# Causal attention in a four-block kernel: from head steps on stacked fp32r halves to query-tile steps of four heads on row groups

## What is computed

```
def _mha(x, y, wq, wk, wv, ..., causal):
    xn = _ln(x, lnx_g, lnx_b)
    yn = _ln(y, lny_g, lny_b)
    q = jnp.einsum('bsc,hcd->bhsd', xn, wq)
    k = jnp.einsum('btc,hcd->bhtd', yn, wk)
    v = jnp.einsum('btc,hcd->bhtd', yn, wv)
    a = jax.nn.softmax(jnp.einsum('bhsd,bhtd->bhst', q, k) * D ** (-0.5), axis=-1)
    if causal:
        mask = (jnp.arange(t)[None, :] > jnp.arange(s)[:, None]).astype(a.dtype)
        a = a * mask
    o = jnp.einsum('bhst,bhtd->bhsd', a, v)
    o = o.transpose(0, 2, 1, 3).reshape(x.shape[0], x.shape[1], H * D)
    x_out = x + o @ li1_w + li1_b
    h = jax.nn.gelu(_ln(x_out, ln3_g, ln3_b) @ li2_w + li2_b, approximate=False)
    return x_out + h @ li3_w + li3_b
```

## Time and profile before

| | us |
|---|---|
| median of 3 runs | 429.45 (426.52 to 430.14) |
| profiled execution, span | 429.6 |
| PE busy | 344.5 (80%) |
| DVE busy | 327.0 (76%) |
| ACT busy | 286.8 (67%) |
| POOL busy | 68.0 (16%) |

### The profile page before, as it was taken

One profiled execution on the slowest core, in us unless ns is written; L12 is line 12 of the kernel. 1 busy time (PEld: TensorE's weight loads), 2 busy tenths in 40 slices (PEclk: granted clock), 3 DMA queues, 4 the chain that ended last, 5 costly groups with the idle time before them and its releaser, 6 DMA issues. The chain is left out here.

```text
span 429.6 us, 6772 instructions
## 1 busy us (share of the span) xinstructions
PE 344.5 (80%) x2037; PEld 238.3 (55%) x2038; DVE 327.0 (76%) x748; ACT 286.8 (67%) x997; POOL 68.0 (16%) x172
## 2 busy tenths in 40 slices
PE   4987898736427877898989978879998599987786
PEld 4755776622312444555546545467577388774756
DVE  3667889878976586899899998974857977876415
ACT  4466988757513786789888888853824789975151
POOL 4200000000020122222232232242111000000000
PEclk9999999995558898999999999989999799999999
DMA  7910000000002663780691384000000000000001
GB/s 234 343 78 0 2 1 0 2 1 0 2 1 72 148 141 82 159 185 1 150 207 37 86 202 106 1 2 0 2 1 2 0 1 2 2 1 2 0 2 49
DMA packets 8859, 24.74 MB, mean 58 GB/s; under 512 B 2667, under 2 KB 2744, under 8 KB 8568
## 3 DMA queue, kind: packets, MB, share of 16 engines
q1 hardware_dynamic: 8824, 24.32, 22.2%
HBM read 7.00 MB, written 0.52 MB: 18 GB/s over the span
## 5 line engine op out<-in xcount | busy, mean ns | idle before, releaser
L1108 ACT ACTIVATE pring<-ps,nm 128x512 f32<-128x512 f32 x128 | 86.8, 686 | 12.2 <-DVE nm L1513 9.8
L1513 DVE TENSOR_REDUCE nm<-ps 128x2 f32<-128x1024 f32 x64 | 77.9, 1219 | 7.5 <-PE ps L633 7.2
L982 ACT ACTIVATE arena<-ps,nmx 128x77 f32<-128x77 f32 x256 | 79.1, 350 | 3.3 <-DVE nmx L1253 3.3
L633 PE MATMUL ps<-Ks,Qs 128*128 128x512 f32 x128 | 48.0, 457 | 16.2 <-ACT pring L1108 12.8
L982 ACT ACTIVATION_READ_ACCUMULATOR arena<-ps,nmx 128x1 f32 x256 | 59.0, 232 | 0.0
L395 PEld LDWEIGHTS ps<-ident,pring 128*128 128x128 f32 x352 | 40.3, 142 | 32.3 <-issue 17.7
L395 PE MATMUL ps<-ident,pring 128*128 128x128 f32 x352 | 52.7, 280 | 5.9 <-ACT xn L1073 3.1
L862 POOL TENSOR_SCALAR_AFFINE_SELECT pring<-pring 128x128 f32<-128x128 f32 x128 | 38.5, 301 | 112.4 <-ACT pring L1108 112.4
L846 POOL TENSOR_TENSOR rstd<-var,minus_half 128x4 f32<-128x4 f32 x18 | 18.2, 1009 | 214.7 <-DVE var L1172 214.7
L1486 DVE COPY arena<-ps 128x384 f32<-128x384 f32 x64 | 39.6, 619 | 9.7 <-PE ps L395 9.3
L467 PE MATMUL ps<-arena,xnT 128*128 128x320 f32 x128 | 40.9, 445 | 4.0 <-ACT arena L982 2.5
(11 more groups left out here) (148 smaller groups left out, 557.9 us busy)
## 6 DMA issues: line engine op xcount, KB each, us to landing
Qs<-qh SPq DMA_DIRECT2D x24, 128.0 KB, 2.4
Qs<-ql SPq DMA_DIRECT2D x24, 128.0 KB, 2.4
Ks<-xo SPq DMA_DIRECT2D x24, 128.0 KB, 2.4
Ks<-xb SPq DMA_DIRECT2D x24, 128.0 KB, 2.4
wa_sb<-in_wa SPq DMA_DIRECT2D x1, 1536.0 KB, 14.3
early<-in_w SPq DMA_DIRECT2D x2, 512.0 KB, 7.6
wa_sb<-in_wa SPq DMA_DIRECT2D x1, 1024.0 KB, 16.5
Qs<-hid SPq DMA_DIRECT2D x16, 64.0 KB, 2.0
```

The costliest lines, as they stand in the source:

```text
L633: m = pe.matmul(bank(res, q), Qs[:, j, b, i * P:(i + 1) * P], Ks[:, j, b, :], start=True, stop=True)
L982: ins = act.activation(Pc[:, i % 2, h * HS:h * HS + M], bank(res, h // 4)[:, h % 4 * HS:h % 4 * HS + M], ACT.Exp, bias=nmx[:, i % 4, h:h + 1],
L1108: ins = act.activation(pring[:, n % 2, i, :], bank(res, q), ACT.Exp, bias=nm1[:, n % 8, i:i + 1], accum_out=den1[:, n % 8, i:i + 1])
L1513: dve.tensor_reduce(nm1[:, n % 8, 2 * u:2 * u + 2], pair(res), AX.X, ALU.max, negate=True).then_inc(nm1_ready, 1)
```

## The change

Heads are no longer stacked. q and k of a group of four heads lie in QT and KT as plain fp32, head h in rows 32h to 32h+31. A step is now one query tile i of a group (again 32 steps, `NSTEP`), and the groups go batch by batch: 0 to 3 are batch 0, 4 to 7 batch 1.

- Scores: `scores(n, u)` are two fp32 matmuls, for heads 2u and 2u+1, each with 32 rows on a row group of its own, 512 columns, each into its own bank. All PSUM banks are single now.
- Only the kept blocks (key block >= query tile) are transposed: 16, 12, 8 and 4 in a group's four steps, in pieces of four blocks, each a whole bank. The pieces alternate between T0 with a copy by ACT and T1 with a copy by DVE.
- Values of step n-2 in every step: 4 - i key blocks of four heads, 128 columns each. `PT_SLOTS` is 3 query tiles of up to 16 blocks.
- The high and low halves and the 128 stacking DMAs are gone; ACT copies q (scaled), DVE copies k, once a group.
- The 1/sums are spread by POOL, and RT and rdx have SBUF of their own.
- Ahead of the loop there are batch 0's transposes, q and k of group 0 and V of batch 0 only. LayerNorm of batch 1 (ln1 and a1) is in steps 0 to 4, V of batch 1 in steps 5 to 8, li1 of batch 0 in step 19, its LayerNorm in steps 20 and 22.
- Cross attention, feed-forwards and gate/up claim, fill and release each bank by itself.

```diff
-PT_SLOTS = 6
+PT_SLOTS = 3
...
-        Qs = sb("Qs", [P, HG, NB, TOK], F32R)
-        Ks = sb("Ks", [P, HG, NB, TOK], F32R)
+        QT, KT = sb("QT", [P, 2, TOK]), sb("KT", [P, 2, TOK])
...
-        BANKS = {"S0": (0, 2), "S1": (2, 4), "T0": (4, 5), "T1": (5, 6), "A": (6, 7), "B": (7, 8)}
+        BANKS = {"S0": 0, "S1": 1, "S2": 2, "S3": 3, "T0": 4, "T1": 5, "A": 6, "B": 7}
...
+        def piece_copy(n, c):
+
+            at = NT * (NT + 1) // 2 * (n // NT) + sum(NT - i for i in range(n % NT)) + c
+            return "T" + str(at % 2), ((pt_act, pt_dve)[at % 2], at // 2 + 1)
...
             def scores(n, u):
 
+                k, b, g, i = step(n)
+                if i == 0 and u == 0:
+                    pe.wait_ge(q_ready, k + 1)
+                    pe.wait_ge(k_ready, k + 1)
+                for h in range(2 * u, 2 * u + 2):
+                    claim(pe, f"S{h}", ("s1", n, h), read_by=(exp1_done, HG * n + h + 1))
+                for h in range(2 * u, 2 * u + 2):
+                    rows_h = slice(h * D1, (h + 1) * D1)
+                    filled(pe.matmul(bank(f"S{h}"), QT[rows_h, k % 2, i * P:(i + 1) * P], KT[rows_h, k % 2, :],
+                                     start=True, stop=True), ("s1", n, h))
+
+            def p_transposes(n, c):
+                res, copied = piece_copy(n, c)
+                blocks = blocks_of(n)[c * NT:(c + 1) * NT]
+
+                pe.wait_ge(masked, HG * n + max(h for h, _ in blocks) + 1)
+                claim(pe, res, ("p1", n, c), read_by=copied)
...
+            def values(n):
...
+                for jb in range(i, NT):
                     for h in range(HG):
...
+                                      PT[:, n % PT_SLOTS, blocks_of(n).index((h, jb)), :],
+                                      start=(jb == i), stop=(jb == NT - 1))
...
+            for n in range(NSTEP + 2):
+                if n < NSTEP:
                     scores(n, 0)
+                if n >= 1 and n <= NSTEP:
+                    for c in pieces(n - 1)[:2]:
+                        p_transposes(n - 1, c)
+                if n < NSTEP:
                     scores(n, 1)
+                if n >= 1 and n <= NSTEP:
+                    for c in pieces(n - 1)[2:]:
+                        p_transposes(n - 1, c)
+                if n >= 2:
+                    values(n - 2)
+                if q_k_projection(n) is not None:
+                    project("qk"[n % NT], q_k_projection(n), "B")
+                if n == 4:
+                    ln_transposes("a1", 1)
+                if value_tile(n) is not None:
+                    project_values(value_tile(n), "B")
+                if n >= NT and n % NT == 0:
+                    sums_transposes(n // NT - 1)
+                if n == NG * NT + 3:
                     li1(0)
```

DVE's loop after the change:

```diff
+            for n in range(NSTEP + 2):
                 for u in range(2):
+                    if n < NSTEP:
+                        for h in range(2 * u, 2 * u + 2):
+                            await_bank(dve, ("s1", n, h))
+                        dve.tensor_reduce(nm1[:, n % 8, 2 * u:2 * u + 2], pair(u), AX.X, ALU.max,
                                           negate=True).then_inc(nm1_ready, 1)
+                    if u == 0 and n >= NT and n % NT == 0:
+                        inverse_sums(n // NT - 1)
+                    if 1 <= n <= NSTEP:
+                        for c in pieces(n - 1)[2 * u:2 * u + 2]:
+                            pt_copy(n - 1, c)
+                if n > NT and n % NT == 1:
+                    normalise(n // NT - 1)
+                if q_k_projection(n) is not None and n % NT == 1:
+                    copy_k(q_k_projection(n))
...
+                if n == 0:
+                    ln_stats("ln1", 1, r)
+                if n == 1:
+                    ln_norm("ln1", 1, r, ("ln1_g", "ln1_b"), x1)
+                if n == 2:
+                    ln_stats("a1", 1, x1)
+                if n == 3:
+                    ln_norm("a1", 1, x1)
```

More of the change, by code:

```diff
@@ L220, in build @@
         f0_done = sem("f0_done")
[L221 to L224, removed]
+        q_ready, k_ready = sem("q_ready"), sem("k_ready")
         V_act, V_dve = sem("V_act"), sem("V_dve")
@@ L358, in unit, with step, blocks_of, pieces @@
             return i // 8, i // 2 % 4, i % 2
[L362 to L387, removed]
+        def step(n):
+            k = n // NT
+            return k, k // NG, k % NG, n % NT
+        def blocks_of(n):
+            return [(h, jb) for h in range(HG) for jb in range(n % NT, NT)]
+        def pieces(n):
+            return range(NT - n % NT)
+        def piece_copy(n, c):
+            at = NT * (NT + 1) // 2 * (n // NT) + sum(NT - i for i in range(n % NT)) + c
+            return "T" + str(at % 2), ((pt_act, pt_dve)[at % 2], at // 2 + 1)
+        def await_pieces(pe, n):
+            for copier in (pt_act, pt_dve):
+                done = [count for _, (who, count) in (piece_copy(m, c) for m in range(n + 1) for c in pieces(m))
+                        if who is copier]
+                pe.wait_ge(copier, max(done))
+        def q_k_projection(n):
+            k, i = n // NT + 1, n % NT
+            return k if k < NGRP and i in (0, 1) else None
+        def value_tile(n):
+            return NT + n - 5 if 5 <= n < 5 + NT else None
         @block.tensor
@@ L604, in _, with project @@
             pe.wait_ge(loaded["wa1"], 16)
-            def project(m):
-                which, b, g = projection(m)
+            def project(which, k, res):
+                b, g = k // NG, k % NG
                 if which == "q":
@@ L613, in project @@
                 w, src = (wa1_sb[:, 0, :], xnT) if which == "q" else (wa1_sb[:, 1, :], ynT)
[L614 to L616 removed]
+                claim(pe, res, (which, k), read_by=(q_ready if which == "q" else k_ready, k + 1))
+                filled(pe.matmul(bank(res), w[:, g * P:(g + 1) * P], src[:, b, :], start=True, stop=True), (which, k))
@@ L1116, in _ @@
+                if q_k_projection(n) is not None and n % NT == 0:
+                    copy_q(q_k_projection(n))
+                if n == 4:
+                    a1_evac(1)
+                if value_tile(n) is not None and value_tile(n) % 2 == 0:
+                    copy_values(value_tile(n))
+                if n >= NT and n % NT == 0:
+                    sums_across(n // NT - 1)
             project_context("a2", 1)
@@ new lines, in _ @@
+                    if 1 <= n <= NSTEP:
+                        for c in pieces(n - 1)[2 * u:2 * u + 2]:
+                            pt_copy(n - 1, c)
+                if n > NT and n % NT == 1:
+                    normalise(n // NT - 1)
+                if q_k_projection(n) is not None and n % NT == 1:
+                    copy_k(q_k_projection(n))
+                if value_tile(n) is not None and value_tile(n) % 2:
+                    copy_values(value_tile(n))
+                if n == 0:
+                    ln_stats("ln1", 1, r)
@@ L1532, in _ @@
                     ln_stats("a1f", 0, xo)
-                if n > HG and n % HG == 3:
-                    normalise(n // HG - 1)
-            ln_norm("a1f", 0, xo)
+                if n == NG * NT + 6:
+                    ln_norm("a1f", 0, xo)
             add_to_xb(1, "li1")
```

381 lines of the change are left out of this document (130 added, 251 removed).

## The result

The changed kernel takes 491.69 us (median of four, 483.85 to 510.26), the kernel before 429.79 beside it. Some executions of a kernel are slower at a lower granted clock, and every ratio in this document counts the others alone, for the changed kernel those of 483.85 and 487.94 us: 1.135 times as long, with a 95% interval of 1.128 to 1.142. The forecast was 446, range 415 to 477: right in direction, short by 45 us of the median and by 40 of the profiled execution, whose span is 486.2 against 429.6.

A forecast was written before the change was run, and what follows sets the result against it. DVE bounds the kernel before; after the change PE's work and waits set the steps. 429.6 + 31.5 (loop) - 7.1 (start) - 7.6 (end) = 446.4 us, range 415 to 477.

The forecast's parts named there:

- Ahead of the loop: Start: scores run right behind batch 0's values, first exp at 138.1 instead of 145.18, a gain of 7.1 us.
- Scores and PE's sum: Attention loop: a two-head burst takes two rounds, 1.15 us, result after 1.08; PE's work sums to 158.5 us, 4.95 a step.
- rival 4: Score matmuls: the row groups do not overlap at all, 501 us; chance 0.05.
- rival 3: Score matmuls: two heads overlap by one instruction only, three rounds, 27.5 us more, 474 us; chance 0.13.
- rival 2: Score matmuls: row groups change tiling at no price, 18.6 us less, 428 us; chance 0.13.
- rival 1: Loop: DVE stays the bound, PE's bursts hide between its waits, 4.06 us a step, 404 us; chance 0.13.
- The walk of four steps: Loop, one group of query tiles: steps of 4.9, 5.3, 5.65 and 5.15 us, sum 21.0, 5.25 a step, 168 us.
- For i=1 PE transposes 16 blocks and projects k: its first scores end at T+0.45: Loop, tile 1: first scores end 0.45 us after the previous step's last exp (T), giving a 5.3 us step.
- Price list of PE, at 2.4 GHz: PE's instruction times from the earlier trace, such as 0.86 us per 512-column fp32 matmul and 0.11 per transpose.
- I take 4: Loop: V projections, batch 1's layer norm and li1, 13 us of work mostly hidden in gaps, add 4 us.
- Behind the loop: End: first feed-forward matmul 10.2 us after the last exp instead of 17.8, ACT late next, a gain of 7.6 us.
- li1 at +3.75: End: the output projection li1 starts 3.75 us after the last exp, where batch 1's started 11.3 behind before.

The follow-up runs named there:

- run 1: Changed kernel with q projected at query tile 2, k at tile 3, V of batch 1 at steps 5, 9, 13 and 17: 472.65 us, ratio 1.1036.
- run 10: Run 1 with batch 1's layer norms, their transposes and evacuations ahead of the loop: 464.13 to 478.78 us, ratio 1.0853 from the first two executions.
- run 4: Changed kernel with all four heads' scores taken from rows 0 to 31, both heads of a burst on one row group: 595.79 us, ratio 1.367.
- run 5: Run 1 with each score matmul over all 128 rows instead of a head's 32 (another output): 487.85 us, ratio 1.135.
- run 11: Run 10 with batch 0's output projection and its layer norm behind the loop: 460.68 us, ratio 1.0726.
- run 9: Run 1 with stacked fp32r scores, low halves after the next step's first maximum, batch 1's norms ahead of the loop, batch 0's output projection behind: 438.69 us.
- Runs 3: Changed kernel with every score matmul over all 128 rows, no row groups, each score a sum over four heads: 496.68 us, ratio 1.157.
- run 12: Kernel before the change, with only POOL instead of DVE copying the sums' reciprocals: 426.97 us, ratio 0.998.

## Why the prediction was right in sign and wrong in size

**Ahead of the loop: right.** The gain is 6.8 for 7.1. Runs 1 and 10 show that some 1.7 of it belong to the place of batch 1's layer norm.

**Scores and PE's sum: right.** Row groups overlap as the column groups did: two rounds for two heads, 1.2 us a burst for 1.15, result after 1.13 for 1.08. Four rounds (rival 4) are run 4, three (rival 3) were nowhere. The Trainium skill (TensorE: Matmul & The Clock Gate, What overlaps and what doesn't) says that matmuls keep program order, which by the prediction would have made rival 3 true. Two rounds were measured, the heads' first instructions 0.01 us apart and their second ones too (run 1), so it adds no round here. Free changes of tiling (rival 2) are excluded by run 1's timeline. DVE as the bound (rival 1) is excluded by its 66 us of idle time.

**The walk of four steps: three tiles right, one wrong.** Tile 3 (4.98 for 5.15), 0 (4.98 for 4.9) and 2 (5.3 to 5.6 for 5.65) came as worked out, tile 1 with 7.25 for 5.3. The step that failed is "For i=1 PE transposes 16 blocks and projects k: its first scores end at T+0.45". It counts what PE issues and leaves out which bank it claims: the sums' transposes ask for B while q stands in it, and q's copy is behind the exp that T marks. I had written that PE gets no wait that it did not have, for the banks of cross attention and the feed-forwards alone; for bank B I never asked. Its removal gave 11.5 us in the profiled loops (204.7 to 193.2) and 13 by the ratios (1.135 to 1.1036). Tile 1 fell to 4.37, but the two projections now stand ahead of tiles 3 and 0, which rose to 5.8 and 5.6, so that a group fell by 1.5 us.

**The clock: missing.** "Price list of PE, at 2.4 GHz" was applied to all 32 steps, because the loop before had 0.99. The changed loop had 0.88. The loop came out 33 us longer than forecast. Where PE is busy throughout, a stretch at half clock costs half its length, so the 51 us cost up to 26; that is an estimate, and by it this is the larger part of the miss. No run takes the half clock away alone. There was a hint in the earlier trace rows: behind a wait, the 32 matmuls of li1 took 5.29 us for batch 0, with 3.4 us of half clock, and 3.84 for batch 1. The Trainium skill (TensorE: Matmul & The Clock Gate, Part 1) says that the clock is set by how busy PE has been and returns under sustained activity. By that rule 2.4 GHz should have come back where PE was busy without a gap. The trace agrees for scores over 128 rows (17.00 of 17.00 us busy at 1.00 in run 5) and disagrees for long stretches on row groups: 1.2 GHz with PE busy 10.20 of 10.20, 17.00 of 17.00 and 23.90 of 23.90 us.

**Work moved into the loop: undersized.** "I take 4" for batch 1's layer norm, V and batch 0's output projection. Without the norm and the projection in it the loop of run 1 fell from 193.2 to 170.2 us. The work itself is 3.8 us of PE and some on DVE; the rest is PE's wait for both, and the half clock behind it, that run 1 has in steps 5 and 21 to 23 and run 11 hasn't. Run 10 says how uneven this is: with only the norm moved, two executions gained, and in two nothing was gained (in the profiled one the clock fell elsewhere). The loop of run 11, with no wait at B and nothing moved in, takes 170.2, where the forecast was 172 with them: what I had worked out was the loop without its waits. That it is so near is in part luck, since the 17 us at half clock in its first steps are offset by last groups of 19.5 to 20.3 us instead of 21.

**Behind the loop: half right.** POOL's memsets and ACT's spreading came as worked out (ACT at +6.0 and to +9.4, forecast +5.8 and +9.3), "li1 at +3.75" did not: it came at +6.0 and took 6.29 us for the 3.84 of the earlier trace rows, at half clock (0.55 in the window above). These two are the 4.7 us, and the last to end is PE's li1, not ACT. Much of the late start is half clock as well: the projection of the context just ahead took 2.42 us, 1.28 before. Past the first feed-forward matmul the kernel needs 127.4 us instead of 126.1, with 5 us more at half clock: so the banks one by one cost or gave nothing that can be told.

**POOL's copy: right**, 0.61 us for 0.8, and nobody waits for it.

**The change taken apart**, by loops: stacked scores in this order, with nothing moved in, 142.2 us (run 9), 2.4 more than before; the same with scores on row groups 170.2 (run 11), 28 more (they also spare ACT and DVE the halves); with layer norm and projection inside 193.2 (run 1); with the wait at B 204.7. The order costs little by itself in the loop; in all, run 9 is 10 us slower than the kernel before, 4.5 of them in a later first exp (149.7). The plain scores make PE the bound (busy 95% of the loop in run 11, 83% in run 9), and a loop bound by PE pays for every wait and for every stretch at a low clock.

What stays open: what makes the clock return under row group matmuls in one stretch or execution and not in the next. Runs 3 and 4 change the rows at the same instructions, but with the rows comes a change of tiling around each burst, and no run separates the two.

## What to carry to other kernels

When a change makes PE the bound, price it at both levels of the clock (1.2 and 2.4 GHz), and ask of each bank that PE claims in order who must read it first and what stands ahead of that reader on its engine. A sum of instructions gives the loop without its waits; a projection or transpose that is "once in four steps" costs its wait, not its time. And where work is moved into a loop to shorten the ends, compare the few microseconds of a seam with what a stall does to a loop that had none.

## What the runs showed of the hardware that was not expected

- With scores on 32 of 128 rows PE can be busy without a gap and stay at the 1.2 GHz level: 23.90 of 23.90 us busy at 0.50 in run 10, 17.00 of 17.00 at 0.52 in run 1, where run 5 with all rows had 1.00. With every score on one row group 235 of 327 us were at 0.50; the same instructions over all rows had 20 of 222. It does not always happen: run 11's row groups kept 0.99 for 153 us.
- Two heads on two row groups take 1.13 us, four on four 1.14, two on one row group about 2.0: row groups overlap in two rounds, as column groups do.
- With PE at the bound, executions of one kernel differ by their granted clock: 0.873 to 0.915 over the span and 464.13 to 478.78 us in run 10, 0.825 to 0.887 and 483.85 to 510.26 us for the changed kernel. The kernel before had 0.927 to 0.948 in its executions beside run 12.
- GpSimd's copy of 128x512 fp32 with a broadcast source took 0.61 to 0.66 us, VectorE's 0.43.
